# A decoder layer on one core: weight loads moved to another queue, three scatters in flight, one root for two norms, zero-padded rows, and five products per expert tile

## The reference

```
x = x + attn(layernorm(x))    # 16 heads, 8 keys at stride 8, ternary weights
x = x + xattn(layernorm(x))   # 64 context rows per sequence, the 54 best scores kept, softmax, W_o
x = x + ffn(layernorm(x))     # below
scores  = sigmoid(x @ gate_w.T) + gate_b;  top 4 of 16 experts, weights normalised
shared  = (silu(x @ w1s) * (x @ w3s)) @ w2s                  # hidden width 176
routed  = sum over the 4 experts e of  weight_e * silu((x @ w1[e]) * (x @ w3[e])) @ w2[e]
out     = shared + routed
```

## Time and profile before

| | us |
|---|---|
| median of 3 runs | 896.58 |
| profiled execution, its own time | 904.63 |
| its span, first to last instruction | 902.5 |
| PE busy | 682.7 (76%) |
| DVE busy | 596.3 (66%) |
| POOL busy | 528.3 (59%) |
| ACT busy | 398.6 (44%) |

### The profile page before, as it was taken

One profiled execution on the slowest core, in us unless ns is written; L12 is line 12 of the kernel. 1 busy time (PEld: TensorE's weight loads), 2 busy tenths in 40 slices (PEclk: granted clock), 3 DMA queues, 4 the chain that ended last, 5 costly groups with the idle time before them and its releaser, 6 DMA issues. The chain is left out here.

```text
span 902.5 us, 18750 instructions
## 1 busy us (share of the span) xinstructions
PE 682.7 (76%) x4138; PEld 555.0 (61%) x4138; DVE 596.3 (66%) x1833; ACT 398.6 (44%) x1053; POOL 528.3 (59%) x419
## 2 busy tenths in 40 slices
PE   0677677676306789798897354999999999899992
PEld 0556566565203555455553123899999998898882
DVE  4899999999112565566455373777677776576662
ACT  0634445351003455446543323655555555455551
POOL 0687877786200126656667661667676656765775
PEclk9988989997757899999999776999999999999997
DMA  6711111200295124343333363568677767675864
GB/s 194 251 37 36 47 35 46 99 23 24 75 255 102 48 73 149 125 138 139 111 109 122 128 201 103 94 113 138 113 131 123 122 112 126 112 125 102 141 113 55
DMA packets 86913, 99.04 MB, mean 110 GB/s; under 512 B 10166, under 2 KB 81654, under 8 KB 86774
## 3 DMA queue, kind: packets, MB, share of 16 engines
q0 software_dynamic: 26736, 37.64, 23.2%
q1 hardware_dynamic: 48992, 51.70, 19.6%
q10 hardware_dynamic: 11094, 8.65, 4.1%
HBM read 49.58 MB, written 52.95 MB: 114 GB/s over the span
## 5 line engine op out<-in xcount | busy, mean ns | idle before, releaser
L1429 POOL DMA_INDIRECT out_dram<-yw,xg x143 | 223.2, 1561 | 129.6 <-issue 56.7
L1036 POOL DMA_INDIRECT xs_scratch<-rows,slot x128 | 127.7, 998 | 84.3 <-DMA xs_scratch<-rows,slot 43.8
L1322 PE MATMUL cbank<-w,stc_hi 88*128 x572 | 116.0, 295 | 2.1 <-DVE stc_lo L1394 0.5
L1322 PE MATMUL cbank<-w_hi,xtc_hi 128*128 x286 | 106.0, 371 | 1.1 <-DVE xtc_lo L1334 0.8
L1322 PEld LDWEIGHTS cbank<-w,stc_hi 88*128 88x128 f32 x572 | 89.5, 189 | 16.6 <-issue 12.2
L1322 PE MATMUL cbank<-w_hi,xtc_lo 128*128 x286 | 93.3, 326 | 0.0
L1322 PE MATMUL cbank<-w,xtc_hi 128*128 x286 | 93.2, 326 | 0.0
L459 PE MATMUL ps_o<-ident,pv 128*128 128x128 f32 x288 | 47.5, 323 | 56.0 <-ACT ot L295 51.8
L1414 DVE TENSOR_SCALAR yw<-cbank,xg 128x256 f32<-128x256 f32 x143 | 69.0, 483 | 30.9 <-PE cbank L1322 21.3
L1334 DVE TENSOR_TENSOR xtc_lo<-cbank,xtc_hi 128x256 fp32r<-128x256 f32 x143 | 60.6, 423 | 38.2 <-ACT xtc_hi L1329 24.8
L1322 PE MATMUL cbank<-w,stc_lo 88*128 x286 | 80.8, 283 | 0.0
(11 more groups left out here) (196 smaller groups left out, 1720.5 us busy)
## 6 DMA issues: line engine op xcount, KB each, us to landing
xg<-xs_scratch SPq DMA_DIRECT2D x143, 144.0 KB
x_in<-x_dram SPq DMA_DIRECT2D x32, 128.0 KB
w_hi<-ctx_t_dram SPq DMA_DIRECT2D x8, 512.0 KB
x_scratch<-u SPq DMA_DIRECT2D x32, 128.0 KB
w_hi<-x_scratch SPq DMA_DIRECT2D x8, 512.0 KB, 5.3
out_dram<-w SPq DMA_DIRECT2D x16, 256.0 KB
w<-w1r_dram ACTq DMA_DIRECT2D x2, 1408.0 KB
w<-w3r_dram ACTq DMA_DIRECT2D x2, 1408.0 KB
```

Source lines behind the costliest of these rows:

```text
L1036: nc.gpsimd.indirect_dma_start(t["xs"], bass.IndirectOffsetOnAxis(ap=slot[:, n % 2, k:k + 1].bitcast(U32), axis=0), rows[:, n % NROW, k // ...
L1322: last = nc.tensor.matmul(out, stationary, moving, start=j == 0, stop=j == len(pairs) - 1)
L1429: nc.gpsimd.indirect_dma_start(t["out"], bass.IndirectOffsetOnAxis(ap=xg[:, p, ID:ID + 1].bitcast(U32), axis=0), yw[:, p % YB, :], None, c ...
```

## The change

- `load_weights` moves from ACT, ahead of its loop, to SP, one piece in each of SP's iterations 0 to 5, behind `load_ct`. The pieces of w2 have another layout (rows 0 to 127 in one half; the last 48 rows twice, at partitions 0 and 64, with zero rows between, in the other).
- `scatter` in the cross phase uses three semaphores in turn (`FLY = 3`).
- One `root` per iteration replaces two: it takes both norms' 128x8 values in one instruction, behind `scatter(2)`.
- `w2rest` and `hsr` get 128 rows, the added ones zero; `th` covers all 128 rows, and `l_t` becomes a product with 16 columns of the identity.
- In the experts the hidden values are transposed as 128 and as 48 + 48 (the last 48 twice). DVE writes the low part of the second copy over its high part, so that one product over 112 rows adds both. y needs 5 products.
- The lists `order` of all four engines are rearranged.

```diff
-REST = HID - P
-HC = HID // 2
+REST, HALF = HID - P, P // 2
+BOTH = HALF + REST
+FLY = 3
...
+        def root(eng, m):
+
+            lo, hi = (0 if m < NG else 1), (2 if m >= 2 else 1)
+            if m < NG:
+                f["stA"].wait(eng, m)
+                f["xhA"].wait(eng, m - 1)
+            if m >= 2:
+                f["stC"].wait(eng, m - 2)
+                f["xhC"].wait(eng, m - 3)
+            f["rs"].sig(nc.gpsimd.tensor_tensor(rstd[:, lo:hi, :], ve[:, lo:hi, :], power[:, lo:hi, :], ALU.pow))
...
-                last = nc.tensor.transpose(R[7][:, LG + k * 2 * NE:LG + (k + 1) * 2 * NE], th[:, k * P:(k + 1) * P],
-                                           ident[0:2 * NE, 0:2 * NE])
+                last = nc.tensor.matmul(R[7][:, LG + k * NE:LG + (k + 1) * NE], th[:, k * P:(k + 1) * P], ident[:, GATES],
+                                        start=True, stop=True)
...
-                    done = n * GT * TOPK // 2 + k // 2
-                    if done:
-                        eng.wait_ge(s_sc[k % 2], 16 * done)
+                    turn, lane = divmod(n * GT * TOPK + k, FLY)
+                    if turn:
+                        eng.wait_ge(s_sc[lane], 16 * turn)
...
+            raw, w2r = keep["w2"][:, 1, :, :, :].bitcast(F32), t["w2r"].rearrange("e p d -> p e d")
+            zeros = t["pads"][0:NE * (HALF - REST), 0:D].rearrange("(p e) d -> p e d", e=NE)
...
+            elif k == 4:
+                eng.dma_start(raw[:, 0, :, :], w2r[0:P, :, :]).then_inc(s_w, 16)
             else:
+                for at in (0, HALF):
+                    eng.dma_start(raw[at:at + REST, 1, :, :], w2r[P:HID, :, :]).then_inc(s_w, 16)
+                    eng.dma_start(raw[at + REST:at + HALF, 1, :, :], zeros).then_inc(s_w, 16)
...
-            t=[(1, sc_mm), (3, sh_mm), (2, t_c), (0, t_a), (1, p_t), (1, y_mm), (2, rest_mm), (0, at_mm(1)), (2, l_t),
+            t=[(1, sc_mm), (2, t_c), (3, sh_mm), (1, p_t), (0, t_a), (1, y_mm), (2, rest_mm), (0, at_mm(1)), (2, l_t),
...
-            g=[(-1, rsA), (3, scatter(2)), (1, rsC), (3, scatter(3)), (2, scatter(0)), (2, scatter(1))])
+            g=[(3, scatter(2)), (-1, root, NG + 2), (3, scatter(3)), (2, scatter(0)), (2, scatter(1))])
...
+                if i < 6:
+                    load_weights(eng, i)
                 if 0 <= i - 3:
                     store_out(1)(eng, i - 3)
...
+            nc.gpsimd.memset(hsr[:, :, :], 0.0).then_inc(s_init, 1)
+            eng.wait_ge(s_init, 4)
...
-            for k in range(6):
-                load_weights(eng, k)
             eng.wait_ge(s_w, 16 * pre.LOADS)
...
-            f["sg"].sig(nc.scalar.activation(sg[:, p % 2, :], hh[:, p % 2, :], ACT.Silu))
+            if n == 0:
+                eng.wait_ge(s_zero, 1)
+            nc.scalar.activation(sg[:, p % 2, 0:P], hh[:, p % 2, 0:P], ACT.Silu)
+            f["sg"].sig(nc.scalar.activation(sg[:, p % 2, P:2 * P].rearrange("p (t h) -> p t h", t=2)[:, :, 0:REST],
+                                             hh[:, p % 2, P:HID].unsqueeze(1).to_broadcast([P, 2, REST]), ACT.Silu))
...
-            f["st_ev"].sig(nc.vector.tensor_tensor(st_lo[:, p % 2, :, :], s_tr(p), st_hi[:, p % 2, :, :].bitcast(F32),
-                                                   ALU.subtract))
+            nc.vector.tensor_tensor(st_lo[:, p % 2, :], s_tr(p)[:, 0, :], st_hi[:, p % 2, 0, :].bitcast(F32), ALU.subtract)
+            f["st_ev"].sig(nc.vector.tensor_tensor(st_hi[HALF:BOTH, p % 2, 1, :], s_tr(p)[HALF:BOTH, 1, :],
+                                                   st_hi[HALF:BOTH, p % 2, 1, :].bitcast(F32), ALU.subtract))
...
-                (x[:, p % 2, half, :], w[:, half, bass.ds(e, 1), :]) for half in range(2)
-                for x, w in ((st_hi, w2_hi), (st_hi, w2_lo), (st_lo, w2_hi))]))
+                (x, w[:, bass.ds(e, 1), :]) for x, w in (
+                    (st_hi[:, p % 2, 0, :], w2_hi[:, 0, :, :]), (st_hi[:, p % 2, 0, :], w2_lo[:, 0, :, :]),
+                    (st_lo[:, p % 2, :], w2_hi[:, 0, :, :]), (st_hi[0:BOTH, p % 2, 1, :], w2_hi[0:BOTH, 1, :, :]),
+                    (st_hi[0:BOTH, p % 2, 1, :], w2_lo[0:BOTH, 1, :, :]))]))
```

More of the change, by code:

```diff
@@ L672, in cross_phase @@
         f_out = [flow(f"fb_out{k}", 32) for k in range(NX2)]
-        s_sc = [sem(f"fb_sc{k}") for k in range(2)]
+        s_sc = [sem(f"fb_sc{k}") for k in range(FLY)]
         f = {n: flow("fb_" + n, per) for n, per in dict(
-            stA=9, rsA=1, nmA=1, xhA=1, at_mm=2, at_ev=2, tA=1, tA_ev=2, bp_mm=1, bp_ev=2,
+            stA=9, rs=1, nmA=1, xhA=1, at_mm=2, at_ev=2, tA=1, tA_ev=2, bp_mm=1, bp_ev=2,
             sc_mm=1, neg=2, top=12, ex=1, pm=4, pt=1, pt_ev=2, y=1, x2=1,
-            stC=9, rsC=1, nmC=1, xhC=1, tC=1, tC_ev=2, lg=1, th=1, lt=1, rt=20, rk=1, rk_in=1, rd=1,
+            stC=9, nmC=1, xhC=1, tC=1, tC_ev=2, lg=1, th=1, lt=1, rt=20, rk=1, rk_in=1, rd=1,
             sh=1, g1=1, hs=1, g1r=1, hsr=1, ys=1, xf=1).items()}
@@ L685, in rows_landed @@
         def rows_landed(eng, n):
-            for s in s_sc:
-                eng.wait_ge(s, 16 * GT * TOPK // 2 * (n + 1))
+            for k in range(FLY):
+                eng.wait_ge(s_sc[k], 16 * len(range(k, GT * TOPK * (n + 1), FLY)))
         tile_table = TileTable(sb, sem)
@@ L731, in apply @@
                 fxh.sig(last)
-            return stats, root, shift, apply
+            return stats, shift, apply
         def transpose_tiles(banks, src):
@@ L929, in th_ @@
             f["lt"].wait(eng, n - 1)
-            f["th"].sig(nc.scalar.activation(th[:, :], R[6][GATES, :], ACT.Tanh, scale=0.5))
+            f["th"].sig(nc.scalar.activation(th[:, :], R[6][:, :], ACT.Tanh, scale=0.5))
         def l_t(eng, n):
@@ L949, in hsr_ @@
             f["ys"].wait(eng, 2 * (n - 2) + 1)
-            f["hsr"].sig(nc.vector.tensor_tensor(hsr[:, n % 2, :], R[6][RESTS, :], g1r[:, :], ALU.mult))
+            f["hsr"].sig(nc.vector.tensor_tensor(hsr[RESTS, n % 2, :], R[6][RESTS, :], g1r[:, :], ALU.mult))
         RT_A, RT_C = 11, 14
@@ L1157, in cross_phase @@
         order = dict(
[L1158 to L1165 removed]
+            t=[(1, sc_mm), (2, t_c), (3, sh_mm), (1, p_t), (0, t_a), (1, y_mm), (2, rest_mm), (0, at_mm(1)), (2, l_t),
+               (0, at_mm(0)), (0, bp_mm), (2, rk_mm), (3, ys_mm(0)), (3, ys_mm(1)), (2, table_mm)],
+            v=[(1, negs), (1, tops), (1, masks), (-1, stA), (3, split_lo(range(0, 4))), (1, x2_), (1, stC),
+               (2, choose), (1, nmC), (-1, nmA), (3, hs_), (3, split_lo(range(4, 7))), (2, shares), (2, spread), (2, hsr_),
+               (3, xf_(0)), (3, xf_(1)), (2, table), (3, split_lo(range(7, NE)))],
+            s=[(1, expo), (2, t_c_ev), (1, p_t_ev), (0, t_a_ev), (3, g1_), (2, th_), (0, at_ev), (2, g1r_), (1, xhC),
+               (-1, xhA), (0, bp_ev), (2, split_hi(range(0, 7))), (3, split_hi(range(7, NE)))],
+            g=[(3, scatter(2)), (-1, root, NG + 2), (3, scatter(3)), (2, scatter(0)), (2, scatter(1))])
         def run(eng, who):
             for i in range(-1, NG + LAST):
[L1169 to L1170 removed]
+                for stage, what, *count in order[who]:
+                    if 0 <= i - stage < (count[0] if count else NG):
                         what(eng, i - stage)
@@ L1379, in s_t @@
             f["st_ev"].wait(eng, n - 2)
-            for half in range(2):
-                last = nc.tensor.transpose(R[4 + p % 2][0:HC, half * P:(half + 1) * P], sg[:, p % 2, half * HC:(half + 1) * HC],
-                                           ident[:, :])
-            f["st"].sig(last)
+            out = s_tr(p)
+            nc.tensor.transpose(out[:, 0, :], sg[:, p % 2, 0:P], ident[:, :])
+            f["st"].sig(nc.tensor.transpose(out[:, 1, :], sg[:, p % 2, P:2 * P], ident[:, :]))
         def s_hi_(eng, n, p):
```

72 lines of the change are left out of this document (31 added, 41 removed).

## The result

The changed kernel took 908.82 us (median of 4 runs, 907.54 to 910.49) where the kernel before took 897.13: ratio 1.0115, interval [1.0064, 1.0165]. It is slower by 1.2%; 860 was forecast. The profiled execution took 907.54 us, its span is 905.6.

What follows compares the result with a forecast made beforehand. Bounds: ACT's issuing queue at the cross phase's start, PE in its middle, POOL at its end and in the experts. Terms -21.2 - 13 - 5 + 3 = -36.2 us from 896.6 gave 860 us; 80% range 848 to 877.

Steps and rivals of the forecast that it cites:

- the one on the pieces: Cross phase: SP's weight pieces, 6 to 9 us each, may slow scatters in iterations 3 to 5, but POOL's slack covers it.
- POOL's slack below: Middle of the cross phase: POOL needs 21.2 us per group, under PE's 24.4, so it doesn't bound there.
- the case that the slack is gone: Cross phase, single root behind 12 scatters: without slack there, every further microsecond goes onto the iteration.
- signs of being wrong: Experts over 5 us shorter, POOL never waiting for `slot` mid cross phase, or a root awaiting scatters while PE is idle.
- Transfers collide: Cross phase rival: weights beside scatters make groups 30 us, losing 17 us over three iterations; 877 us, chance 0.11.
- "slower" rival: Cross phase: root behind 12 scatters, norms and products behind it; at 2.2 us per scatter +25, about 921 us; chance 0.04.
- Start: Start of the cross phase: weights issued by SP let DVE's first norm begin at 245.8; -21.2 us, bounds -19 and -22.
- PE: Cross phase: iteration 24.4 us instead of 26.4; 2.4 us in each of five iterations and 1 in iteration 2; -13 us.
- POOL's tail: End of the cross phase: group 5's first scatter to the next phase 73.5 us instead of 78.3; -5 us, bounds 0 and -9.
- Experts: Expert phase: five products give 0, as POOL has a backlog; the first 16 tiles cost +3 us, bounds 0 and +6.

Runs made afterwards that it cites:

- a_third: The changed kernel, unchanged, run again on chip 7: 877.33 us, 0.9808 of the kernel before.
- a_up2: The changed kernel with all six weight pieces issued by SP ahead of its first ct load, on chip 9: 856.63 us, 0.9542 of the kernel before.
- b_spload: The kernel before with only the weight loads moved to SP, one piece per iteration, on chip 11: 896.39 us, 1.0018 of the kernel before.
- b_five: The kernel before with only the changed kernel's expert phase and w2 layout, on chip 11: 902.33 us, 1.0071 of the kernel before.
- a_act2: The changed kernel with the weight loads back on ACT ahead of its loop, on chip 9: 884.94 us, 0.9859 of the kernel before.
- b_fly3: The kernel before with three scatters in flight and nothing else, on chip 7: 887.37 us, 0.9932 of the kernel before.

## Why the prediction was wrong

**The step that failed** is the one on the pieces: "A piece can slow scatters in iterations 3 to 5; POOL's slack below covers that." It priced them at nothing. They cost 20.6 us of intervals (a_third against a_up2). The slack was not there: 21.2 of 24.4 us left out the waits for earlier scatters, 2.3 to 3.0 us per period even without pieces, and had the root at 1.04 us where eight columns take 1.67. Measured, POOL's period in a_up2 is 24.3 to 24.9 us without a wait for `slot`. So every wait beside a piece went onto the intervals by way of the root, DVE's `hs_` and PE, as the prediction had said for the case that the slack is gone. Two of its signs of being wrong were there: POOL never waits for `slot` in the middle, and a root waits for scatters while PE is idle. The length of the pieces was wrong too: "6 to 9 us" came from 241 GB/s at a time when no scatter ran; the last piece took 18.

**The rival was right, at quiet chips.** "Transfers collide" was given 877 us and 0.11, with slow scatters, the single root late and three iterations with pieces. a_third measured 877.3 and 20.6 us for the 17. That the total fits to 0.3 us is luck: over half of the loss lies in one interval and not a third in each of three, and other terms came out better than forecast. The Trainium skill ("Trainium Kernel Development and Optimization", rules on engines and DMA) had said what the rival was built on: transfers of all queues run on the same 16 engines, another queue saves issue time only. The runs agree: b_spload has its first copy of `slot` 21.2 us earlier and loses 21.2 in intervals. Its weak point as a rival was my counter-argument, that a piece lasts a quarter of an iteration.

**No step covered the late signals.** They cost up to 32 us (908.8 or 909.6 against 877.3, a comparison between chips; the kernel before is itself 5 to 12 us slower on chips 3 and 14 than on 9 and 7), on chips 3 and 14 and on that of the first result, not on 7, 9 and 11. The "slower" rival named slow scatters behind one root; that is not what happens in the fifth and sixth interval, where no engine waits for POOL by the program. The trace of before showed little of it (a `y_mm` wait of 3.61 us at 367.25) and I had not looked for a signal later than its producer.

The other terms held in size, on a quiet chip:
- *Start*, forecast -21.2 us: -22.4 at the first `slot` copy.
- *PE*, forecast a period of 24.4 us instead of 26.4: measured 24.3 to 24.9 (a_up2) against 26.4 (b_five). But that is POOL's period as much as PE's, so the agreement is in part luck. The first five intervals give -12.9 where -13 was forecast, in another split: -4.7 in the first, where 1 was forecast, and about 2 in each of the others. The last two, which belong to the tail, give -2.6. The products of `ys_mm` are 0.43 us apart where rows are padded (402.23, 402.67, 403.10 below), which were 0.63 apart. The Trainium skill ("TensorE: Matmul & The Clock Gate", on LDWEIGHTS) says that a weight load's time goes by its columns and not its rows. The trace of before agrees for the load itself, 0.30 us for two of 128 rows and 0.29 for two of 48 (below). That padding would bring nothing did not follow: it removed the 0.33 us between loads whose row count changes. `l_t` takes 0.96 us, forecast 0.9.
- *POOL's tail*, forecast -5: besides that -2.6, last copy to first accumulate 53.4 us (a_act2) against 58.2 (b_five), -4.8. The third scatter in flight can give it alone: b_fly3, with nothing else changed, has 51.1.
- *Experts*, forecast 0 and +3: the five products bring nothing, as POOL has a backlog; the first accumulates cost +4.0 (and three more transfers on ACT's queue 4.3, in kernels that load there).

PE's weight loads of `ys_mm` before, where the row count alternates:

```profile
428.09 0.30 PEld L1069 LDWEIGHTS bank<-w2s,hs 128*128 128x128 f32 x2
428.72 0.29 PEld L1070 LDWEIGHTS bank<-w2rest,hsr 48*128 48x128 f32 x2 [0.33 <-issue]
```

PE of a_up2, products of `ys_mm` and the next `l_t`:

```profile
402.23 0.59 PE L1079 MATMUL bank<-w2rest,hsr 128*128 128x256 f32 x2
402.67 0.59 PE L1078 MATMUL bank<-w2s,hs 128*128 128x256 f32 x2
403.10 0.59 PE L1079 MATMUL bank<-w2rest,hsr 128*128 128x256 f32 x2
...
417.92 0.96 PE L945 MATMUL bank<-identb,th 128*128 128x16 f32 x8
```

The sum of the terms was -36.2 us. a_up2, which is the change without the collision, on a chip without late signals, is -40.9 against before beside it.

## What to carry to other kernels

A background transfer is free only while nothing in an ordered queue waits for another transfer beside it: put it where no such transfer runs, even if that means issuing all of it at once and early. The slack of an in-order engine is its period less its busy time, its gaps and its waits for transfers; look in the trace whether it ever waits for its input at all. And a change that packs an engine's queue without pauses should be measured on several chips and at several times, since its gain may be there in some only.
